# Moving a GpSimd product, a mask, a carry copy and three groups of matmul jobs to other points of a 64-point schedule in a state-space scan kernel

## What is computed

```python
xr, gate = jnp.split(x @ W_in.T, 2, axis=-1)
xr = xr + t_emb[:, None, :]
xc = silu(depthwise_conv4(xr) + b_conv)
xn = layernorm(xc) * ln_g + ln_b                       # 1024 channels
Bm, Cm, dt = jnp.split(xn @ W_xproj.T, 3, axis=-1)
Ad = 1.0 + tanh(dt @ W_dt.T + b_dt) * 0.01 * A
Bd = Bm * jnp.minimum(norm(xn), 1.0)
h = clip(h * ad + bd * xt, -10, 10);  yt = einsum(ct, h)  # scan over the tokens, 16 states
y = ys + D * xn
x = x + (y * silu(gate)) @ W_out.T
```

## Time and profile before

| what | value |
| --- | --- |
| median of 3 runs | 2055.43 us (2054.57 to 2057.09) |
| the profiled execution | 2052.24 us |
| its span, first to last instruction | 2050.5 us |
| mean granted TensorE clock | 0.988 |
| busy: PE, DVE, ACT, POOL | 1826.6, 1637.6, 1376.2, 1753.4 us |

### The profile page before, as it was taken

One profiled execution on the slowest core, in us unless ns is written; L12 is line 12 of the kernel. 1 busy time (PEld: TensorE's weight loads), 2 busy tenths in 40 slices (PEclk: granted clock), 3 DMA queues, 4 the chain that ended last, 5 costly groups with the idle time before them and its releaser, 6 DMA issues.

```text
span 2050.5 us, 46002 instructions
## 1 busy us (share of the span) xinstructions
PE 1826.6 (89%) x16240; PEld 1396.0 (68%) x16240; DVE 1637.6 (80%) x2109; ACT 1376.2 (67%) x3462; POOL 1753.4 (86%) x1476
## 2 busy tenths in 40 slices
PE   5689998899999899999898999899999899899888
PEld 4466776676776676676676777676677676677655
DVE  3478887888887888888887888788888788888786
ACT  5577666777666776766676766676766677766643
POOL 1489988889988889988889988889988889988886
PEclk9799999999999999999999999999999999999999
DMA  5222222222222222222222222222222222222221
GB/s 178 58 69 54 70 58 74 63 78 59 67 58 75 62 79 59 67 57 77 62 77 59 67 63 71 62 75 59 69 72 62 64 73 61 67 75 58 62 67 29
DMA packets 168069, 139.14 MB, mean 68 GB/s; under 512 B 100704, under 2 KB 137968, under 8 KB 163168
## 3 DMA queue, kind: packets, MB, share of 16 engines
q1 hardware_dynamic: 167840, 136.20, 24.9%
HBM read 62.07 MB, written 9.31 MB: 35 GB/s over the span
## 4 chain that ended last, share of the span: by engine, by line
PE 29%; POOL 25%; issue 19%; ACT 15%; DVE 8%; SPq 2%; DMA 1%; POOLq 0%; DVEq 0%; ACTq 0%
POOL prod L1094 17%; PE ps_y L590 6%; ACT tap L750 5%; PE ps_job L517 5%; PE ps_job L483 4%; DVE ks L995 4%; PE ps_fill L573 3%; PE ps_fill L564 3%; ACT low L793 3%; PE ps_job L496 2%; POOL xn L1039 2%; POOL xn L1042 2%; PE ps_job L490 2%; SPq L406 1%; ACT xh L688 1%
## 5 line engine op out<-in xcount | busy, mean ns | idle before, releaser
L1094 POOL TENSOR_TENSOR prod<-ks,crep 128x512 f32<-128x512 f32 x1024 | 1286.0, 1274 | 142.1 <-DVE ks L995 140.4
L995 DVE TENSOR_TENSOR_SCAN ks<-low,ps_fill 128x512 f32<-128x512 f32 x1024 | 1208.3, 1208 | 227.0 <-PE ps_fill L573 226.7
L793 ACT COPY low<-ps_fill 128x512 f32<-128x512 f32 x1024 | 584.6, 580 | 477.0 <-PE ps_fill L564 474.4
L590 PE MATMUL ps_y<-c_sb,prod 128*128 128x128 f32 x4096 | 613.4, 275 | 9.9 <-ACT xc L758 7.1
L590 PEld LDWEIGHTS ps_y<-c_sb,prod 128*128 128x128 f32 x4096 | 457.5, 142 | 75.9 <-issue 27.1
L573 PE MATMUL ps_fill<-spans,pick 128*128 128x512 f16 x1024 | 390.7, 381 | 76.4 <-ACT low L793 71.8
L564 PEld LDWEIGHTS ps_fill<-ts,xs 128*128 128x128 f16 x4096 | 315.8, 98 | 171.8 <-issue 10.7
L564 PE MATMUL ps_fill<-ts,xs 128*128 128x128 f16 x4096 | 397.9, 220 | 9.2 <-DMA xs<-h 7.6
L750 ACT ACTIVATE tap<-xr,cols_sb 128x128 f32<-128x128 f32 x768 | 251.9, 393 | 0.0
L478 PE MATMUL ps_job<-x,w_in 128*128 128x128 f16 x3072 | 215.9, 221 | 10.3 <-POOL x L1064 7.8
L483 PE MATMUL ps_job<-w_in,x 128*128 128x512 f16 x768 | 202.0, 379 | 21.3 <-ACT gate L682 21.3
(11 more groups left out here) (124 smaller groups left out, 1962.7 us busy)
## 6 DMA issues: line engine op xcount, KB each, us to landing
crep<-c_dram SPq DMA_DIRECT2D x32, 1024.0 KB, 4.7
xs<-xh SPq DMA_DIRECT2D x256, 64.0 KB, 2.0
xs<-xl SPq DMA_DIRECT2D x224, 64.0 KB, 2.0
xf<-in_xT SPq DMA_DIRECT2D x32, 256.0 KB, 2.8
res<-in_x SPq DMA_DIRECT2D x32, 256.0 KB, 2.8
out_dram<-res SPq DMA_DIRECT2D x32, 256.0 KB, 2.3
ts<-tth SPq DMA_DIRECT2D x128, 32.0 KB
ts<-tth SPq DMA_DIRECT2D x128, 31.0 KB
```

The source lines that it names most:

```text
L590: last = mm(ps_y[:, cut], prod[:, (TILES * k + s) % HOLD, e, :], ident, start=False, stop=(u % 4 == 3 and q == 3 and e == QN - 1), is_tran ...
L793: copy(low[:, (TILES * k + s) % RING], ps_fill[:, (TILES * k + s) % RING]).then_inc(sem["low_copied"], 1)
L995: nc.vector.tensor_tensor_scan(ks[:, u % 2, QN * q:QN * (q + 1)].rearrange("d n t -> d (n t)"), low[:, g % RING], ps_fill[:, g % RING], 0. ...
L1094: tt(prod[:, g % HOLD], ks[:, u % 2, part], crep[:, p, part], ALU.mult).then_inc(sem["weighed"], 1)
```

## The change

In the tables, `gate` 1 goes from point 8 to 9 (taken at 13, not 12), `xr` 0 from 19 to 16 (taken at 20, not 22), `xr` 1 from 25 to 22 (taken at 26, not 29). The tap blocks go from 24, 28, 30, 34, 38, 40, 43, 46 to 21, 24, 28, 33, 38, 41, 44, 47. ScalarE's `lend` copy moves one point behind the `ch` copy, so VectorE's L971 no longer waits for it; `lend` waits for `carry_taken` in its place, and the next user of that PSUM bank waits for `lend_set`. ScalarE's `bqm[1]` goes from point 27 to 29. GpSimd's second half of D * xn goes from s = 11 to s = 22 and the mask `ttl` from s = 18 to s = 21. SP's program is the same.

```diff
-                (7, 1, "yT", 1, -1, 2, 1), (8, 4, "gate", 1, 0, 2, 0),
-                (15, 1, "zT", 0, 1, 1, 1), (19, 4, "xr", 0, 2, 2, 0),
-                (25, 4, "xr", 1, 2, 2, 0), (19, 1, "bd", 0, 1, 1, 1), (26, 1, "nb", 0, 1, 1, 1),
+                (7, 1, "yT", 1, -1, 2, 1), (9, 4, "gate", 1, 0, 2, 0),
+                (15, 1, "zT", 0, 1, 1, 1), (16, 4, "xr", 0, 2, 2, 0), (19, 1, "bd", 0, 1, 1, 1),
+                (22, 4, "xr", 1, 2, 2, 0), (26, 1, "nb", 0, 1, 1, 1),
...
-        TAKE = {("z", 0): 5, ("gate", 0): 7, ("hend", 0): 6, ("yT", 1): 8, ("gate", 1): 12,
-                ("zT", 0): 15, ("bd", 0): 20, ("xr", 0): 22, ("nb", 0): 26,
-                ("xr", 1): 29, ("carry", 0): 31, ("carry", 1): 36, ("conv", 0): 44, ("out", 0): 55,
+        TAKE = {("z", 0): 5, ("gate", 0): 7, ("hend", 0): 6, ("yT", 1): 8, ("gate", 1): 13,
+                ("zT", 0): 15, ("bd", 0): 20, ("xr", 0): 20, ("nb", 0): 26,
+                ("xr", 1): 26, ("carry", 0): 31, ("carry", 1): 36, ("conv", 0): 44, ("out", 0): 55,
...
-        TAP_AT = [24, 28, 30, 34, 38, 40, 43, 46]
+        TAP_AT = [21, 24, 28, 33, 38, 41, 44, 47]
...
-                    pe.wait_ge(sem[name + "_taken"], (kk + off) * per + i + 1)
+                    freed = "lend_set" if name == "carry" else name + "_taken"
+                    pe.wait_ge(sem[freed], (kk + off) * per + i + 1)
...
                     copy(ch[:, half], bank("carry", i)).then_inc(sem["carry16"], 1)
+                for i in range(2):
+                    if point != TAKE["carry", i] + 1 or not exists(k, 1):
+                        continue
+                    half = slice(i * BANK, (i + 1) * BANK)
+                    act.wait_ge(sem["carry_taken"], 2 * (k + 1) + i + 1)
                     if exists(k, 0):
                         act.wait_ge(sem[f"lend_in{p}"], 16 * pair(k, p, 0))
                     copy(lend[:, half], bank("carry", i)[0:NS]).then_inc(sem["lend_set"], 1)
-                if point == 27 and exists(k, 1):
+                if point == 29 and exists(k, 1):
...
                     dve.wait_ge(sem[f"xstack_in{q}"], N_XSTACK * pair(k, p, 1))
-                    dve.wait_ge(sem["lend_set"], 2 * j + i + 1)
...
                         pool.wait_ge(sem["xn_done"], k + 1)
+                        skipped(p, 0)
+                    if s == 22 and exists(k, 0):
                         since(pool, "yT_in1", N_YT * k)
-                        for i in range(2):
-                            half = slice(i * BANK, (i + 1) * BANK)
-                            tt(xd[i], xn[:, p, half], row_d[:, half], ALU.mult).then_inc(sem["xd_done"], 1)
+                        skipped(p, 1)
...
-                    if s in (14, 18) and exists(k, 1):
-                        h = s // 4 - 3
+                    if s in (14, 21) and exists(k, 1):
+                        h = s // 21
...
+            def skipped(p, i):
+
+                half = slice(i * BANK, (i + 1) * BANK)
+                tt(xd[i], xn[:, p, half], row_d[:, half], ALU.mult).then_inc(sem["xd_done"], 1)
```

## The result

The changed kernel takes 2169.34 us (median of 4 runs, 2166.15 to 2171.02) against 2055.0 us: a ratio of 1.0556, 95% interval 1.0537 to 1.0575. It is slower by 114 us; 84 were forecast, and a time of 2139 us in a range of 2090 to 2170. The profiled execution took 2166.15 us with a span of 2164.3 us.

What follows compares the result with a forecast made beforehand. A chain of ScalarE's blocks, the carry halves, VectorE's `gated` and TensorE's `base` was taken to set the pace. Stack copies +100, carry chain -34, start +1.6, clock +16 gave +84 us: 2139 us, range 2090 to 2170.

Steps and rivals of the forecast that it cites:

- two slower rivals: Clock falling in every chunk (chance 0.13) and new waits in the middle of the period (chance 0.14), each 2173 us.
- the start: First pass on ScalarE: a tap block now stands ahead of the bounds, before the first mask; +1.6 us once.
- The mask: `ttl` ends 5.2 us later, SP's copies follow, TensorE's next first fill waits 3.1 us a chunk; about +100 us.
- The lend copy: VectorE's L971 no longer waits for ScalarE's `lend` copy at the second half; -0.5 us a chunk.
- bqm, xr and the taps: Blocks fill ScalarE's 1.77 us wait for `nbl`, partly given back; -0.6 us a chunk, bounds +0.5 to -2.8.
- The clock: TensorE's clock falls after one in three of 31 waits, 1.6 us each; +16 us, bounds 0 and +50.
- One of the three waits: In the kernel before, one of three first-fill waits for copies was followed by TensorE's clock at 1.2 GHz.
- The D half: 1.27 us of GpSimd work moves from a full stretch to an idle one; costed at nothing.
- The middle gets worse: Rival: new waits for the input's low part, the bank and `bqm[1]` add +0.5 us a chunk; 2173 us, chance 0.14.
- The clock falls in every chunk: Rival: every new TensorE wait is followed by 1.2 GHz, 50 us in place of 16; 2173 us, chance 0.13.

Runs made afterwards that it cites:

- e1: The changed kernel with the mask `ttl` back at s = 18, all other parts kept: 2069.95 us, ratio 1.0085.
- g12: The changed kernel with 12 matmuls of no use ahead of the first fill's waits for the stacks: 2158.51 us, ratio 1.0510.
- e9: The kernel before with the mask `ttl` at s = 21 and 12 matmuls of no use ahead of the first fill's waits: 2151.02 us, ratio 1.0476.
- e3: The kernel before with only the mask `ttl` moved, from s = 18 to s = 20: 2071.16 us, ratio 1.0091.
- e4: The changed kernel with SP issuing the eight `tth` copies after the first mask, waiting for `ttl` only before its four: 2068.98 us, ratio 1.0077.
- g11: The kernel before with the `lend` copy's change and the new tables with `bqm` at point 29; mask and D half as before: 2072.07 us, ratio 1.0091.
- g14: The kernel before with D's second half at s = 22, second `lend` copy two points behind `ch`, new tables, `bqm` at point 27: 2031.48 us, ratio 0.9890.
- g13: The kernel before with D's second half at s = 22 and only the second `lend` copy moved, two points behind `ch`: 2047.07 us, ratio 0.9968.
- e8: The kernel before with only the second half of D * xn moved to s = 22: 2049.78 us, ratio 0.9979.
- e2: The kernel before with only the mask `ttl` moved, from s = 18 to s = 21: 2189.85 us, ratio 1.0668.

## Why the prediction was right, point by point

Direction and main cause were right, the sum was not. 2169.34 us is inside 2090 to 2170 by 0.7 us, 30 us above the forecast 2139 and outside the 2090 to 2155 that I gave the forecast itself. The range held only because it reached up over most of two slower rivals; that is luck. The runs split the 114 us, by ratio:

| part | forecast | measured | from |
| --- | --- | --- | --- |
| all but the mask: `lend`, `bqm`, `xr`, taps, D half, the start | -32 | +17 | e1 |
| the mask's wait, clock at full | +100 | +87 | e1 to g12 |
| the falls of the clock | +16 | +10 | g12 to the changed kernel |

The first row is wrong by 50 us, and the other two hid 20 of it.

- *The mask.* Forecast: end 5.2 us later, way to the fill 15.5 us, 3.1 us of wait in each chunk, about 100 us. Measured: 3.1 us between the two distances, the mask's end to the fill 15.4 to 15.7 us, waits of 2.6 to 2.9 us in the steady part and 94.0 us in all. Alone and with the clock at full it costs 0.0476 of the ratio, 98 us (e9). e1, e3 and e4 show each link: the mask's place, the slack of 2.1 us, the issues.
- *The lend copy* (-0.5) *and bqm, xr and the taps* (-0.6). This term failed. It was -34 us in the sum; the two together cost 0.8 us a chunk without the mask's wait (e1, g11), and with it 0.25 ahead of `y_summed`. The size of the single marks was right: `xr` waits for its input (0.43 us) and its bank (0.62), `bqm` ends about 2.9 us later, and behind the second `ch` copy 0.5 us were won. Two prices were left out or too small. The wait added ahead of `lend` stands at nothing in the sum: I named what VectorE no longer waits for and not what stands behind the waiting copy on ScalarE, which waits 1.04 and 0.81 us a chunk there. The late `bqm` was to cost ScalarE 0.5 us; it made TensorE wait 1.51 us, and with `bqm` at point 27 the new tables gain 0.45 us a chunk (g14 against g13).
- *The clock.* Forecast: a fall at one wait in three, at 1.6 us each, +16 us. It was about +10 us: 11 falls at the 28 steady waits, as forecast, each at half the price. The price is not fixed: 0.8 us in the changed kernel, 1.0 in e8 (a period of 62.60 us against 61.58 in the kernel before, with the same waits), 1.6 at 148.78. "One of the three waits" in the prediction leaves one out: the granted clock was at 0.50 from 89.00 to 95.83 too, beside the wait of 3.06 us at 89.32, so it was two of three, though near the start of the run. The page "TensorE: Matmul & The Clock Gate" of the Trainium skill (HAM oscillation — how this bites in real kernels) describes a kernel whose clock falls behind the DMA wait of every single pass. e2 agrees, 28 of 28; the changed kernel does not, 11 of 28.
- *The D half.* Costed at nothing; right for the period, and 4 us at the two ends of the run were missed.
- *The rivals.* "The middle gets worse" was nearest: with `lend`'s -0.5 it put the two terms together at 0 and the time at 2173 us, 4 us over the measured one. It had a chance of 0.14. "The clock falls in every chunk" came about in e2, not in the changed kernel.

Check of the sum against the spans (2164.3 - 2050.5 = 113.8). The 28 periods between the third first fill and the last but one are 103.8 us longer: 77.9 of waits for DMAs, 28 x 0.25 = 7 ahead of `y_summed`, 28 x 0.3 = 9 since TensorE comes to the fill later behind it, and some 10 from the falls of the clock. The other 10 us lie in the first and last chunks, where the waits for DMAs grew from 7.6 to 16.1.

## What to carry to other kernels

Before an instruction is put off, follow what it releases through the issuing queue to the first wait at its end, and compare the shift with the slack there: the slack is free and all beyond it is paid in full. A wait that is taken from one engine and given to another costs what stands behind it in that engine's queue, and parts that are neutral alone must be timed together. If a late producer is needed, let the queue issue first what doesn't depend on it.

## What was not expected of the hardware

A wait of 3 us in each pass cost up to 39 us more than itself through TensorE's clock (e2 against e9), and matmuls of no use in the wait brought that back. In the kernel before, waits of 1.1 to 1.5 us, several in each period, had left the clock at full in all steady periods of the trace. One was longer, 1.86 us for `y_summed`, in its trace and in that of e8: in e8 the granted clock was 0.50 for 3.4 us behind it (from 1112.20) and the period 62.6 us long, in the kernel before it stayed at full.
